# One transformer layer with 64 experts: where the turned x1 is split into high and low parts

## What is computed

```python
x = layernorm(x + attn(x, W_K, W_Q, W_V, W_O))         # this is x1
scores = softmax(x @ gate_w.T); gate_vals, idx = top_k(scores, 6)
# each expert: its first 128 rows, in the order of the tokens
h = silu(einsum('ecd,eid->eci', xe, w1)) * einsum('ecd,eid->eci', xe, w3)
ye = einsum('eci,edi->ecd', h, w2)
routed = (ye[fe, pc] * keep * gate_vals).sum over the 6 choices
z = silu(x @ sw1.T) * (x @ sw3.T) @ sw2.T              # the shared part, 704 wide
out = layernorm(x + routed + z)
```

## Time and profile before

| | us |
|---|---|
| three runs | 2707.1, 2709.0, 2712.7 |
| median | 2709.0 |
| profiled execution | 2708.8 |
| its span, first to last instruction | 2707.1 |

### The profile page before, as it was taken

One profiled execution on the slowest core, in us unless ns is written; L12 is line 12 of the kernel. 1 busy time (PEld: TensorE's weight loads), 2 busy tenths in 40 slices (PEclk: granted clock), 3 DMA queues, 4 the chain that ended last, 5 costly groups with the idle time before them and its releaser, 6 DMA issues. The chain is left out here.

```text
span 2707.1 us, 48261 instructions
## 1 busy us (share of the span) xinstructions
PE 2489.2 (92%) x14304; PEld 2153.1 (80%) x14304; DVE 1781.2 (66%) x3826; ACT 1455.3 (54%) x3250; POOL 252.2 (9%) x209
## 2 busy tenths in 40 slices
PE   6999999999999999999999999789458999999992
PEld 5888888888888888888888887677347999999992
DVE  4665665665566466466466566688647887787885
ACT  3554555555455455456456455443246766666662
POOL 0000000000000000000000000154411212121120
PEclk8999999999999999999999999899778999999996
DMA  6311311311311310320320210677277999999996
GB/s 241 120 54 41 120 48 47 116 48 51 116 48 46 106 62 18 109 88 15 105 95 15 87 64 8 238 248 252 87 241 228 299 292 275 291 294 270 298 294 184
DMA packets 177955, 382.89 MB, mean 141 GB/s; under 512 B 19673, under 2 KB 52569, under 8 KB 167456
## 3 DMA queue, kind: packets, MB, share of 16 engines
q1 hardware_dynamic: 155104, 333.12, 36.6%
q0 software_dynamic: 20288, 42.59, 6.9%
q10 hardware_dynamic: 2304, 4.20, 0.4%
HBM read 282.11 MB, written 106.35 MB: 143 GB/s over the span
## 5 line engine op out<-in xcount | busy, mean ns | idle before, releaser
L403 ACT ACTIVATE pT_hi<-turned 128x512 fp32r<-128x512 f32 (+3 forms) x640 | 331.0, 537 | 310.2 <-PE turned L626 309.0
L497 DVE TENSOR_TENSOR pT_lo<-turned,pT_hi 128x512 fp32r<-128x512 f32 (+3 forms) x640 | 376.6, 606 | 100.9 <-ACT pT_hi L403 100.3
L392 ACT ACTIVATE probs<-bank,neg_max 128x512 f32<-128x512 f32 (+3 forms) x640 | 396.0, 626 | 80.7 <-DVE neg_max L491 76.9
L483 DVE TENSOR_REDUCE max_part<-bank 128x1 f32<-128x512 f32 (+2 forms) x576 | 347.7, 622 | 107.9 <-PE bank L609 99.1
L596 PE MATMUL bank<-x_sb,w_hi 128*128 128x512 f32 x1024 | 327.9, 402 | 20.0 <-ACT ident_bf L367 13.5
L626 PE MATMUL turned<-ident,probs 128*128 128x128 f32 x2176 | 322.6, 275 | 19.7 <-issue 19.1
L626 PEld LDWEIGHTS turned<-ident,probs 128*128 128x128 f32 x2176 | 264.5, 141 | 65.0 <-issue 20.7
L641 PE MATMUL z_ps<-pT_hi,v_hi 128*128 128x512 f32 (+3 forms) x640 | 255.2, 399 | 15.7 <-DVE pT_lo L497 12.9
L1510 DVE TENSOR_TENSOR up_lo<-w_raw,up_hi 128x704 fp32r<-128x704 f32 x262 | 222.8, 889 | 56.1 <-ACT up_hi L1397 52.9
L609 PE MATMUL bank<-k_lo,q_hi 128*128 128x512 f32 (+2 forms) x640 | 254.0, 397 | 0.0
L609 PE MATMUL bank<-k_hi,q_hi 128*128 128x512 f32 (+2 forms) x640 | 250.3, 391 | 0.0
(11 more groups left out here) (177 smaller groups left out, 4972.1 us busy)
## 6 DMA issues: line engine op xcount, KB each, us to landing
w_raw<-in_w SPq DMA_DIRECT2D x262, 352.0 KB, 5.9
x_sb<-x_parts SPq DMA_DIRECT2D x62, 1024.0 KB, 6.1
w_raw<-in_w SPq DMA_DIRECT2D x128, 256.0 KB, 5.7
rows_in<-gathered_x SPq DMA_DIRECT2D x65, 263.5 KB, 5.5
gathered_x<-empty_row SPq DMA_DIRECT2D x64, 263.5 KB, 9.3
z_dram<-z_sb SPq DMA_DIRECT2D x64, 256.0 KB, 2.9
z_raw<-z_dram SPq DMA_DIRECT2D x16, 1024.0 KB, 6.5
w_raw<-in_w_qkv SPq DMA_DIRECT2D x32, 384.0 KB, 10.0
```

Source lines behind the costliest of these rows:

```text
L392: nc.scalar.activation(probs[:, u % 2, r, kc * CHUNK:kc * CHUNK + used], bank[:, job_at["s", h, c, r, kc] % BANKS, 0:used], ACT.Exp, bias= ...
L403: nc.scalar.activation(pT_sb[0][:, n % TURNS, lo_col:], turned[:, n % TURNS, lo_col:], ACT.Copy).then_inc(turn_hi, 1)
L483: nc.vector.reduce_max(max_part[:, row % ROWS, kc:kc + 1], bank[:, job % BANKS, 0:used], axis=AX_X).then_inc(part_done, 1)
L497: nc.vector.tensor_tensor(pT_sb[1][:, n % TURNS, lo_col:], turned[:, n % TURNS, lo_col:], pT_sb[0][:, n % TURNS, lo_col:].bitcast(F32), AL ...
```

## The change

The routing no longer splits. ACT's only copy of t_ps is x1T, in full float32; SP stores that, 256 KB a tile, to x1T_dram when ACT has written it (t_read). PE's next turn waits for t_read. x1T_hi, x1T_lo and their semaphores are gone. In the experts, SP loads a whole tile into the new buffer sT_raw, in the step before the one ahead of the unit "s" that opens a tile: steps 0 and 6. In steps 1 and 7 ACT copies it to the high part of sT and DVE subtracts for the low part, both ahead of the step's first three weight pieces; PE's unit waits for DVE's sT_lo. There is one sT_raw, free again after DVE's split. The rest is unchanged; line numbers below the first edit shift.

```diff
 def project_and_route(...):                         # routing
-        xT_part = [sb(f"x1T_{n}", [P, 2, DT, P], F32R) for n in ("hi", "lo")]
...
@@ SP, step(i, k)
-                    sp.wait_ge(t_split, done(i, k - 1))
-                    for part in range(2):
-                        sp.dma_start(x1T_parts[bass.ds(t, 1), part].rearrange("a p n -> (a p) n"),
-                                     xT_part[part][:, (k - 1) % 2].rearrange("p t n -> p (t n)").bitcast(F32)
-                                     ).then_inc(t_stored[(k - 1) % 2], 16)
+                    sp.wait_ge(t_read, done(i, k - 1))
+                    sp.dma_start(x1T_dram[bass.ds(t, 1)].rearrange("a p n -> (a p) n"),
+                                 x1T[:, (k - 1) % 2].rearrange("p t n -> p (t n)")).then_inc(t_stored[(k - 1) % 2], 16)
...
@@ ACT, turned(i, k)
                     act.wait_ge(l_ready, done(i, k - 2))
+                    act.wait_ge(t_stored[k % 2], i * (16 * NB // 2) + 16 * (k // 2))
                 nc.scalar.activation(x1T[:, k % 2].rearrange("p t n -> p (t n)"), t_ps[:], ACT.Copy
                                      ).then_inc(t_read, 1)
-                if exists(i, k - 2):
-
-                    act.wait_ge(t_stored[k % 2], i * (32 * NB // 2) + 32 * (k // 2))
-                nc.scalar.activation(xT_part[0][:, k % 2].rearrange("p t n -> p (t n)"), t_ps[:], ACT.Copy
-                                     ).then_inc(t_hi, 1)
...
@@ PE, turn(i, k)
-                    pe.wait_ge(t_split, done(i, k - 1))
+                    pe.wait_ge(t_read, done(i, k - 1))
...
@@ DVE, step(i, k)
-            def split_x1T(i, k):
-                dve.wait_ge(t_hi, done(i, k))
-                if exists(i, k - 2):
-
-                    dve.wait_ge(t_stored[k % 2], i * (32 * NB // 2) + 32 * (k // 2))
-                nc.vector.tensor_tensor(xT_part[1][:, k % 2].rearrange("p t n -> p (t n)"), t_ps[:],
-                                        xT_part[0][:, k % 2].rearrange("p t n -> p (t n)").bitcast(F32),
-                                        ALU.subtract).then_inc(t_split, 1)
...
-                if exists(i, k - 1):
-                    split_x1T(i, k - 1)
...
 def experts(...):
         eT = [sb(f"eT_{n}", [P, 2, DT * P], F32R) for n in ("hi", "lo")]
+        sT_raw = sb("sT_raw", [P, DT * P])
         sT = sb("sT", [P, 2, 2, DT * P], F32R)
...
+        tile_of_step = {unit_of["s", 2 * s] - 1: s for s in range(NS // 2)}
...
@@ SP
-                    if kind == "s" and n % 2 == 0:
-                        s = n // 2
-
-                        back = unit_of["s", (2 * s - 3) % NS] - (NU if s < 2 else 0)
-                        sp.wait_ge(up_ready, after(i, NU, back + 1))
-                        for part in range(2):
-                            sp.dma_start(sT[:, s % 2, part].bitcast(F32),
-                                         x1T_parts[bass.ds(i * (NS // 2) + s, 1), part].rearrange("a p n -> (a p) n")
-                                         ).then_inc(sT_loaded[s % 2], 16)
+                    if u + 1 in tile_of_step:
+                        s = tile_of_step[u + 1]
+
+                        sp.wait_ge(sT_lo, after(i, NS // 2, s))
+                        sp.dma_start(sT_raw[:], x1T_dram[bass.ds(i * (NS // 2) + s, 1)].rearrange("a p n -> (a p) n")
+                                     ).then_inc(sT_loaded, 16)
...
@@ ACT
+            def split_tile(i, s):
+                back = unit_of["s", (2 * s - 3) % NS] - (NU if s < 2 else 0)
+                act.wait_ge(up_ready, after(i, NU, back + 1))
+                act.wait_ge(sT_loaded, i * (16 * NS // 2) + (16 * s + 16))
+                nc.scalar.activation(sT[:, s % 2, 0], sT_raw[:], ACT.Copy).then_inc(sT_hi, 1)
...
                     loads = [pieces.index(piece) for piece in pieces_of_step[u]]
+                    if u in tile_of_step:
+                        split_tile(i, tile_of_step[u])
                     for q in loads[:3]:
                         split_piece(i, q)
...
@@ DVE (called at the same place)
+            def split_tile(i, s):
+                dve.wait_ge(sT_hi, i * (NS // 2) + (s + 1))
+                nc.vector.tensor_tensor(sT[:, s % 2, 1], sT_raw[:], sT[:, s % 2, 0].bitcast(F32),
+                                        ALU.subtract).then_inc(sT_lo, 1)
...
@@ PE, up(i, u, first_body)
-                    pe.wait_ge(sT_loaded[s % 2], i * (32 * NS // 4) + (32 * (s // 2) + 32))
+                    pe.wait_ge(sT_lo, after(i, NS // 2, s + 1))
...
@@ post_ln_layer
-    x1T_parts = dram("x1T_parts", [TILES, 2, P, DT * P])
+    x1T_dram = dram("x1T_dram", [TILES, P, DT * P])
```

More of the change, by code:

```diff
@@ L688, in _, with project_and_route @@
             body(PAIRS - 1, True)
-def project_and_route(nc, z_dram, w_o, gate_w, x_rows, sums_dram, x1T_parts, gathered_x):
+def project_and_route(nc, z_dram, w_o, gate_w, x_rows, sums_dram, x1T_dram, gathered_x):
     BIG = 1 << 20
@@ L772, in project_and_route @@
         t_read = sem("t_read")
-        t_hi = sem("t_hi")
-        t_split = sem("t_split")
         t_stored = [sem(f"t_stored{n}") for n in range(2)]
@@ L864, in _ @@
             for n in range(2):
-                sp.wait_ge(t_stored[n], 32 * TILES // 2)
+                sp.wait_ge(t_stored[n], 16 * TILES // 2)
         @block.scalar
@@ L1144, in newton, with experts @@
     step(nc.vector.tensor_copy(s[:, 2:3], s[:, 9:10]))
-def experts(nc, gathered_x, x1T_parts, w13, w2, s13, s2, sums_dram):
+def experts(nc, gathered_x, x1T_dram, w13, w2, s13, s2, sums_dram):
     with ExitStack() as ctx:
@@ L1242, in experts @@
         rows_loaded = [sem(f"rows_loaded{n}") for n in range(2)]
-        sT_loaded = [sem(f"sT_loaded{n}") for n in range(2)]
+        sT_loaded = sem("sT_loaded")
+        sT_hi = sem("sT_hi")
+        sT_lo = sem("sT_lo")
         t_ready = sem("t4_ready")
@@ L1479, in _ @@
             dve.sem_inc(ys_read, NS // 2)
+            dve.sem_inc(sT_lo, NS // 2)
             dve.sem_inc(gate_ready, NE)
@@ L1798, in post_ln_layer @@
     sums_dram = dram("sums_dram", [SEQ + P, DM])
-    x1T_parts = dram("x1T_parts", [TILES, 2, P, DT * P])
+    x1T_dram = dram("x1T_dram", [TILES, P, DT * P])
     attention(nc, xT, x_parts, w_qkv, z_dram, gathered_x, sums_dram)
-    project_and_route(nc, z_dram, w_o, gate_w, x_rows, sums_dram, x1T_parts, gathered_x)
-    experts(nc, gathered_x, x1T_parts, w13, w2, s13, s2, sums_dram)
+    project_and_route(nc, z_dram, w_o, gate_w, x_rows, sums_dram, x1T_dram, gathered_x)
+    experts(nc, gathered_x, x1T_dram, w13, w2, s13, s2, sums_dram)
     combine(nc, sums_dram, out)
```

## The result

The changed kernel takes **2697.29 us** (median of 5 runs, 2694.83 to 2700.76) against 2709.04 us of the kernel before (5 runs, 2704.99 to 2712.65): a ratio of 0.9962, 95% interval 0.9951 to 0.9974. It is faster by 11.75 us; 8.3 had been forecast. The profiled execution spans 2698.5 us, 8.6 less than that of before.

The account below looks back on a forecast made before the run. VectorE's list was taken to bound the routing and TensorE the experts' stage; -9.2 + 0.7 + 0 + 0.4 - 0.2 = -8.3 us from 2708.8 gave 2700.5 us, own bounds 2697 to 2704, wider range 2695.5 to 2706 (about 0.85).

Parts of the forecast that it names:

- VectorE's list sets the routing's pace: Routing: removing x1T_lo from VectorE's list saves 0.61 us in 15 of 16 tiles, 9.2 us; the first brings nothing.
- GpSimd, +0.7: Routing: GpSimd, behind in early tiles, gives back 0.7 us (bounds 0 and 9.2); it waits for VectorE from tile 9.
- rival (a): Routing: GpSimd stays behind to the end and gives back half of VectorE's gain; 2704.4 us, chance 0.13.
- The splits hidden: Experts, steps 1 and 7: added ScalarE and VectorE work costs nothing under TensorE's matmuls; 20.9 us without that cover.
- (c): Experts, steps 1 and 7: the split holds TensorE up; if counted in full +20.9 us, 2721.4 us, chance 0.04.
- Starts of bodies, +0.4: Experts, seven body starts: the step 0 load delays w_raw pieces by 0.82 us; 0.4 us taken, bounds 0 and 5.7.
- (b): Experts, body starts: with the 1.25 us of room used up, each costs the whole 0.82 us; 2705.8 us, chance 0.07.
- The first body, -0.2: Experts, first body: one transfer fewer, -0.82 us, against two new operations, +0.6; sum -0.2, bounds -1.5 and +1.5.
- (d): Experts: transfers bound the stage, so the halved loads bring 14.5 us more; 2686.0 us, chance 0.05.
- (e): Experts: GpSimd's scatters, stretched by the new subtractions, come to bind; 10.9 us, 2711.4 us, chance 0.01.

Follow-up runs that it names:

- split3: Changed kernel with VectorE's split done three times over in each of 14 places in the experts' stage: 2707.3 us, 1.0001 of the kernel before.
- traffic2: Changed kernel with the kernel before's traffic (each tile stored twice, a second load beside each shared-part load): 2699.36 us, 0.9967 of the kernel before.
- the second: The changed kernel unaltered, run again beside the kernel before: 2699.26 us against 2706.31 us.
- the third: The changed kernel unaltered, run once more beside the kernel before: 2696.99 us against 2709.17 us.

## Why the prediction was right

The time lay 3.2 us below the forecast and within the range, and it was right for its reason. Of these 3.2 us, 1.4 are the change's (9.7 where 8.3 had been forecast); the rest belongs to this pair of runs.

- **VectorE's list sets the routing's pace: right.** -9.2 forecast, -9.0 in the first pair and 9.7 between the means. The term was sized by a tile at 0.87 us; six of fifteen stand at 0.96 to 0.98, with a register operation for the wait on the store. The change takes that wait off VectorE's list too, 0.04 us a tile on average, for which the prediction had no term. The first tile brought nothing, as said: VectorE now waits 5.22 us for TensorE's o_ps there, 0.94 before.
- **GpSimd, +0.7: no delay found.** It caught up at tile 12, not 9, but it waits 4.41 us for VectorE at tile 14, where its scatters start 9.05 us earlier in the routing than before, so rival (a) is out.
- **The splits hidden: right**, to the number: 0.23 us left idle forecast, 0.24 measured in steps 7 (0.31 in steps 1); split3 gives 1.0 us of room in all, and (c) is out. TensorE's 196.79 us of 200 is unchanged.
- **Starts of bodies, +0.4 with a longer wait of ScalarE: the size was near, the mechanism absent.** I took the late pieces for full transfers (1.06, 321 GB/s). But SyncE had stood still for 6 us just before, and was catching up. In the changed kernel that gap is gone, the same stretch (2322 to 2330 us) shows a share of 0.78 at 215 GB/s, and all of ScalarE's waits for w_raw behind the first body are gone too. In traffic2, where a load stands at step 0 and the gap is back, the longest wait is 2.5 us, near the 2.7 forecast; h_sb of that body's start stands 0.9 us later, and 0.1 us of it is left at step 95: (b) is out.
- **The first body, -0.2: open in size, no gain shown.** The pair gave -2.4 us for all that follows the routing, but step 6 of the first body moves by 3.0 us between two profiles of the kernel before and by 3.9 between three of the changed one, against my bounds of 1.5.
- **Rivals (d) and (e): out.** The page of after reads 4.2 MB less from HBM (277.91 for 282.11) and the steady bodies keep their length to 0.05 us; GpSimd is busy 40.47 of 200 us, 41.73 before.

The whole was 11.75 us in the first pair, 7.1 in the second and 12.2 in the third, 10.3 on average. Differences of several us outside the routing, from run to run, are as large as the distance of these from its 9.7.

## What to carry to other kernels

Where one engine's in-order list sets the pace, an instruction is worth the time between its neighbours' starts, the register operations of its wait included; average that over the tiles rather than read one. The same instruction is free on another engine, or in another stage, up to that stage's idle time plus what the bound engine does before it needs the result: put the work in twice or three times to measure that room. Before a pair of profiles is read as cause and effect, profile the same kernel again and compare stage by stage.

## What the hardware showed that I hadn't expected

- Two DMAs fewer in a loop of 68 removed a stop of SyncE of 5.4 to 7.8 us at the loop's ends; 24 semaphore increments more didn't bring it back. The stop lies right behind the loop's branch (5.4 us from it to the next instruction, at 2324.4), and instruction packets land in it.
- Computing the value of a wait inside a loop costs VectorE's list some 0.1 us: 0.96 to 0.98 us from start to start in the six tiles with a register operation, 0.87 or 0.88 in the nine without.
- VectorE's small operations change their length between executions of the same code: in the routing the mean of the normalisation (x<-y) is 610 ns in one profile of the changed kernel and 599 in another, the cast to chosen_bf 246 and 202 ns. The routing of these two is 264.1 us all the same; what moves it between 262.7 and 264.1 us is open.
- The first body of the experts' stage differs by up to 3.9 us between executions of one kernel, with TensorE's granted clock between 0.81 and 1.00 in the same 8 us.
